# A woven scan and feed-forward stage: weights in eight spaced pieces, two GELUs and a spare square root, other banks and block order

## The reference

```
def step(S, inp):                       # 64 chunks of 16 tokens, per head, D = 16
    kh = k @ S;  target = v - k
    kh_hat = (kh - mean(kh)) * rsqrt(var(kh) + EPS)
    g = w * kh_hat + b - target;  gw = g * w
    v_new = (gw - mean(gw) - kh_hat * mean(gw * kh_hat)) * rstd
    A = tril(q @ k.T) * eta
    qh = q @ S - A @ v_new
    o = q + layernorm(qh, w, b)
    S = S - (k * eta).T @ v_new
x = x + rmsnorm(o * sigmoid(gate)) * norm_w @ Wo
x = x + (gelu(x @ Wg.T) * (x @ Wu.T)) @ Wd.T     # MLP_DIM 2048, x of 2048 tokens
```

## Time and profile before

| | us |
|---|---|
| median of 3 runs (lowest, highest) | 3264.78 (3262.69, 3271.79) |
| profiled execution, its own time | 3264.96 |
| its span, first to last instruction | 3262.9 |

### The profile page before, as it was taken

One profiled execution on the slowest core, in us unless ns is written; L12 is line 12 of the kernel. 1 busy time (PEld: TensorE's weight loads), 2 busy tenths in 40 slices (PEclk: granted clock), 3 DMA queues, 4 the chain that ended last, 5 costly groups with the idle time before them and its releaser, 6 DMA issues. The chain is left out here.

```text
span 3262.9 us, 69524 instructions
## 1 busy us (share of the span) xinstructions
PE 2505.6 (77%) x25665; PEld 1674.5 (51%) x25752; DVE 2174.5 (67%) x4949; ACT 1820.7 (56%) x3501; POOL 851.8 (26%) x870
## 2 busy tenths in 40 slices
PE   7788869878888787676776777699987035888889
PEld 3333327533333663344443444478865034777789
DVE  7488886758785766898998999743335335555552
ACT  3398864324445432898998999632223002666664
POOL 2233333200000412454554555200002101222223
PEclk9899989869999888899999999899988555888889
DMA  3533311253231224222201220030000794112210
GB/s 124 124 65 64 64 66 50 91 90 53 42 37 15 96 93 110 32 27 28 27 11 19 27 27 1 9 152 1 1 14 11 157 193 53 25 26 31 38 27 11
DMA packets 300472, 173.95 MB, mean 53 GB/s; under 512 B 206961, under 2 KB 265345, under 8 KB 297857
## 3 DMA queue, kind: packets, MB, share of 16 engines
q1 hardware_dynamic: 290560, 156.69, 24.2%
q10 hardware_dynamic: 9600, 13.13, 1.3%
HBM read 113.84 MB, written 51.51 MB: 51 GB/s over the span
## 5 line engine op out<-in xcount | busy, mean ns | idle before, releaser
L1279 ACT ACTIVATE ad_e<-ps,ad_nm 128x1024 f32<-128x1024 f32 (+7 forms) x512 | 384.2, 758 | 92.6 <-DVE ad_nm L1340 90.5
L1340 DVE TENSOR_REDUCE ad_nm<-ps 128x1 f32<-128x1024 f32 (+7 forms) x512 | 369.2, 749 | 49.6 <-PE ps L1210 49.0
L1313 POOL TENSOR_TENSOR ad_e<-ad_e,ad_c 128x128 f32<-128x128 f32 (+7 forms) x256 | 293.3, 1146 | 15.1 <-DVE ad_rz L1353 8.7
L1208 PE MATMUL ps<-ad_k_st,ad_q_st 96*128 96x512 bf16 (+3 forms) x768 | 211.8, 336 | 91.9 <-ACT ad_e L1279 49.5
L615 ACT ACTIVATE ab_e<-ps 128x512 f32<-128x512 f32 (+3 forms) x384 | 167.6, 490 | 204.7 <-PE ps L532 158.8
L1364 DVE CUSTOM_DVE_ANT_0 ad_t<-ad_e,ad_rz 128x128 f32<-128x128 f32 (+7 forms) x256 | 224.0, 875 | 3.7 <-ACT ad_pr L1287 2.5
L365 PE MATMUL ps<-warm,ident_b 128*128 128x512 bf16 x425 | 137.4, 389 | 114.5 <-ACT ad_prT L1264 112.1
L1306 POOL TENSOR_TENSOR ad_e<-ad_e,later_k 128x128 f32<-128x128 f32 x256 | 118.7, 464 | 374.5 <-ACT ad_e L1279 374.5
L1898 POOL TENSOR_TENSOR st_it_low<-st_it,st_it_high 128x256 fp32r<-128x256 f32 x128 | 95.3, 745 | 416.0 <-ACT st_it_high L2069 371.1
L1287 ACT ACTIVATE ad_pr<-ad_t,ad_low 128x128 f32<-128x128 f32 (+7 forms) x256 | 200.7, 784 | 0.0
L1223 PE MATMUL ps<-ident,ad_pr 128*128 128x128 f32 x1152 | 174.0, 279 | 24.5 <-ACT ad_pr L1287 24.5
(11 more groups left out here) (387 smaller groups left out, 7097.7 us busy)
## 6 DMA issues: line engine op xcount, KB each, us to landing
aa_q_st<-scr_a SPq DMA_DIRECT2D x48, 256.0 KB, 6.2
split<-f_split SPq DMA_DIRECT2D x16, 768.0 KB, 3.9
ad_q_st<-scr_d SPq DMA_DIRECT2D x48, 256.0 KB, 9.7
g_w<-split SPq DMA_DIRECT2D x8, 1536.0 KB, 18.5
st_w<-split ACTq DMA_DIRECT2D x8, 1536.0 KB, 21.7
scr_a<-pa_parts SPq DMA_DIRECT2D x24, 384.0 KB, 2.5
scr_d<-pd_parts SPq DMA_DIRECT2D x20, 384.0 KB, 2.5
aa_k_st<-scr_a SPq DMA_DIRECT2D x48, 128.0 KB, 6.5
```

The source lines that it names most:

```text
L1208: last = pe.matmul(m.ps[:, bank, 0:n], q_st[:, b, 2 * h + s, t * P:(t + 1) * P], k_st[:, b, s, cc * QB:cc * QB + n], start=True, stop=True)
L1279: act.activation(e[:, u % EB, s, 0:L], src, ACT.Exp, bias=nm[:, u % EB, s:s + 1], accum_out=z[:, u % EB, s:s + 1]).then_inc(exped[s], 1)
L1313: pool.tensor_tensor(e[:, k, 1, 0:L], e[:, k, 1, 0:L], c[:, k:k + 1].to_broadcast([P, L]), ALU.mult).then_inc(mixed, 1)
L1340: dve.tensor_reduce(nm[:, u % EB, s:s + 1], src, AX.X, ALU.max, negate=True).then_inc(maxed[s], 1)
```

## The change

`DENSE` goes from 21 to 19 and block work moves to lags 5 to 12. The weights are issued one piece every second step, from step 3 on. Both GELUs of a step follow each other, behind the scan's square root; a spare square root of a constant (`keep_table`) follows them. The roots of the block work stand next to a square root. On the PE the order is gate, gate, up, down, up, and `project_down(1)` comes ahead of the scan's key product; banks and their waits follow that order. On DVE `finish` comes first in its step, and the odd multiply moves from ahead of `gradient` to just ahead of `advance`. `statistics` is cut out of `add_rows` and comes late in the step. `wo` and `norm_w` are loaded behind the first scan inputs, with their own semaphore.

```diff
-    DENSE = 21
+    DENSE = 19
...
+    kept_root = ph.sb("kept_root", [P, 1])
...
-    bank_of = lambda product: 3 + product % 3
+    bank_of = lambda r, part: 3 + (4 * (r // 2) + 2 * part + r % 2) % 3
...
-    sp.dma_start(wo[:], a["wo_t"].rearrange("(k p) n -> p k n", p=P)).then_inc(w_loaded, 16)
-    sp.dma_start(g_row[:], a["norm_w"].rearrange("(k x) -> k x", k=2).partition_broadcast(P)).then_inc(w_loaded, 16)
+    sp.dma_start(wo[:], a["wo_t"].rearrange("(k p) n -> p k n", p=P)).then_inc(wo_loaded, 16)
+    sp.dma_start(g_row[:], a["norm_w"].rearrange("(k x) -> k x", k=2).partition_broadcast(P)).then_inc(wo_loaded, 16)
...
-    pool.wait_ge(w_loaded, 48)
+    pool.wait_ge(wo_loaded, 32)
...
-    in_turns(pool, [(DENSE + 1, remainder(1)), (14 - 7, at_block_end(gain_and_base)), (15 - 7, at_block_end(weigh)),
-                    (DENSE, remainder(0))], NCH)
+    in_turns(pool, [(6, at_block_end(gain_and_base)), (6, at_block_end(weigh)),
+                    (DENSE, remainder(0)), (DENSE, remainder(1))], NCH)
...
-        if part == 0:
-            reach(pe, gated, r - 1)
+        if (part, r % 2) == (0, 0):
+            reach(pe, gelued, r)
+        elif (part, r % 2) == (0, 1):
+            reach(pe, gated, r - 2)
+        elif (part, r % 2) == (1, 0):
+            reach(pe, gated, r)
-            out = m.ps[:, bank_of(2 * r + part), 0:TB]
+            out = m.ps[:, bank_of(r, part), 0:TB]
...
-    def gate_even(n):
-        hidden(2 * n, 0, gate)
-    def up_even(n):
-        hidden(2 * n, 1, up)
-    def both_odd(n):
-        hidden(2 * n + 1, 0, gate)
-        hidden(2 * n + 1, 1, up)
+    def first_product(odd):
+        return lambda n: hidden(2 * n + odd, 0, gate)
+    def second_product(odd):
+        return lambda n: hidden(2 * n + odd, 1, up)
...
+        if j == 0:
+            pe.wait_ge(wo_loaded, 32)
...
-    pe.wait_ge(w_loaded, 48)
-    in_turns(pe, [(2, update), (2, within_chunk), (DENSE, gate_even), (1, state_keys), (1, state_queries), (0, early),
-                  (17 - 7, at_block_end(project_out)),
-                  (DENSE, up_even), (DENSE + 2, project_down(1)), (DENSE, both_odd), (DENSE + 1, project_down(0)),
-                  (16 - 7, at_block_end(turn_rows)), (19 - 7, at_block_end(turn_normed))], NCH)
+    in_turns(pe, [(2, update), (2, within_chunk), (DENSE + 2, project_down(1)),
+                  (1, state_keys), (1, state_queries), (0, early),
+                  (8, at_block_end(turn_rows)), (9, at_block_end(project_out)),
+                  (DENSE, first_product(0)), (DENSE, first_product(1)), (DENSE, second_product(0)),
+                  (DENSE + 1, project_down(0)), (DENSE, second_product(1)),
+                  (11, at_block_end(turn_normed))], NCH)
...
-            act.activation(ge[:, r % 2, :], m.ps[:, bank_of(2 * r), 0:TB], ACT.Gelu_apprx_tanh).then_inc(gelued, 1)
+            act.activation(ge[:, r % 2, :], m.ps[:, bank_of(r, 0), 0:TB], ACT.Gelu_apprx_tanh).then_inc(gelued, 1)
...
+    def load_weights(n):
+        if n % 2 == 0 and n // 2 < MLP // C:
+            act.dma_start(w[:, n // 2].bitcast(F32), a["split"][n // 2]).then_inc(w_in[n // 2], 16)
+    def keep_table(n):
+        reach(act, table_kept, n)
+        act.activation(kept_root[:], eps[:, 0:1], ACT.Sqrt).then_inc(table_kept, 1)
-    for c in range(MLP // C):
-        act.dma_start(w[:, c].bitcast(F32), a["split"][c]).then_inc(w_in[c], 16)
-    in_turns(act, [(2, copy), (13 - 7, at_block_end(square_rows)), (15 - 7, at_block_end(square_again)),
-                   (20 - 7, at_block_end(keep_high_x)),
-                   (DENSE, gelu(0)), (1, square), (1, square_root), (DENSE + 1, keep_high(1)), (DENSE, gelu(1)),
-                   (DENSE, keep_high(0)),
-                   (13 - 7, at_block_end(root_rows)), (15 - 7, at_block_end(root_again)), (16 - 7, at_block_end(copy_rows)),
-                   (18 - 7, at_block_end(root_x)), (19 - 7, at_block_end(scale_second))], NCH)
+    in_turns(act, [(2, copy), (5, at_block_end(square_rows)),
+                   (1, square), (1, square_root), (7, at_block_end(root_again)), (11, at_block_end(scale_second)),
+                   (DENSE, gelu(0)), (DENSE, gelu(1)), (DENSE, keep_table),
+                   (5, at_block_end(root_rows)), (10, at_block_end(root_x)), (6, at_block_end(square_again)),
+                   (DENSE, keep_high(0)), (DENSE, keep_high(1)),
+                   (8, at_block_end(copy_rows)), (11, at_block_end(keep_high_x)),
+                   (3, load_weights)], NCH)
...
-    dve.wait_ge(w_loaded, 48)
+    dve.wait_ge(w_loaded, 16)
...
-            dve.tensor_tensor(it[:, r % 2, :], ge[:, r % 2, :], m.ps[:, bank_of(2 * r + 1), 0:TB],
+            dve.tensor_tensor(it[:, r % 2, :], ge[:, r % 2, :], m.ps[:, bank_of(r, 1), 0:TB],
...
+    def statistics(j):
...
-    in_turns(dve, [(13 - 7, at_block_end(sum_rows)), (14 - 7, at_block_end(normalise_rows)), (15 - 7, at_block_end(sum_again)),
-                   (16 - 7, at_block_end(size_rows)), (18 - 7, at_block_end(add_rows)), (19 - 7, at_block_end(scale_first)),
-                   (20 - 7, at_block_end(keep_low_x)),
-                   (1, receive), (1, variance), (DENSE + 1, multiply(1)), (1, gradient), (0, mask),
-                   (DENSE + 2, at_block_end(finish)), (DENSE, multiply(0)), (1, advance)], NCH)
+    in_turns(dve, [(DENSE + 2, at_block_end(finish)), (6, at_block_end(normalise_rows)), (7, at_block_end(sum_again)),
+                   (8, at_block_end(size_rows)), (10, at_block_end(add_rows)), (11, at_block_end(scale_first)),
+                   (12, at_block_end(keep_low_x)),
+                   (1, receive), (1, variance), (1, gradient), (DENSE, multiply(0)), (0, mask),
+                   (5, at_block_end(sum_rows)), (10, at_block_end(statistics)),
+                   (DENSE, multiply(1)), (1, advance)], NCH)
```

More of the change, by code:

```diff
@@ L1778, in scan_and_ffn @@
     it_low = ph.sb("it_low", [P, 4, TB], F32R)
-    made, cleared, w_loaded = ph.sem("made"), ph.sem("cleared"), ph.sem("w_loaded")
+    made, cleared, w_loaded, wo_loaded = ph.sem("made"), ph.sem("cleared"), ph.sem("w_loaded"), ph.sem("wo_loaded")
     rows_in = [ph.sem(f"rows_in{k}") for k in range(len(EDGES) - 1)]
@@ L1795, in scan_and_ffn @@
                                                         ph.sem("n_scaled_a"), ph.sem("n_turned"))
-    x_high_in, x_low_in = ph.sem("x_high_in"), ph.sem("x_low_in")
+    x_high_in, x_low_in, table_kept = ph.sem("x_high_in"), ph.sem("x_low_in"), ph.sem("table_kept")
     gate, up, gelued, gated = ph.sem("gate"), ph.sem("up"), ph.sem("gelued"), ph.sem("gated")
```

## The result

The changed kernel takes 3188.88 us (median of 4 runs, 3187.07 to 3195.24) against 3268.28 of the kernel before (4 runs); the ratio is 0.9761, 95% interval 0.9737 to 0.9785: 79 us faster. Forecast were 3160 us and a range of 3120 to 3212. The execution profiled took 3195.24 us, its span is 3193.2.

The account below looks back on a forecast made before the run. Losses were put less in the plain step than in block work and the clock, with the PE as the bound afterwards. Middle part -82, tail -6.5 and weights -18 sum to -106.5 from 3264.96: 3160 us, 8 in 10 within 3120 to 3212.

Parts of the forecast that it names:

- (b): Woven steps: the chain bounds and the plain step stays 6.95 us; 3190 us, chance 0.20 together with (e).
- (e): Only block work (finish and roots) gains, plain step and early part stay; 3192 us, chance 0.20 together with (b).
- Plain step: Woven step without block work: falls from 6.95 to 6.3 us, the PE becoming the bound.
- Woven part: The 46 steps from 18th to 64th state advance: 337 against 419.4 us, -82; 58.6 us a block including clock.
- 0.7 for small waits: Term in the woven part's block sum of 56.6 us: 0.7 us a block for small waits.
- Weights: First part of the stage: spaced weight pieces and earlier rows give -18 us, bounds -31 and 0.
- I keep 10 of the 13 us: First part: 10 us of loss for weights remains with spaced pieces, since the traffic is the same.
- 2 relay: First part: 2 us of loss left for the relay, the 14.81 us step shrinking to 5 to 7.
- Tail: Dense work after the scan: -8.6 for two fewer steps, +4 as ACT bounds, -2 for block roots; -6.5 us.
- (a): Woven steps: the clock stays low for half of them, 67 us instead of 11.5; 3215 us, chance 0.16.
- (c): First part: ACT is held by its own weight issues, 120 us; 3280 us, chance 0.05 together with (d).
- (d): Woven part and tail: ACT drains at each table switch, 122 us more; 3282 us, chance 0.05 together with (c).

Follow-up runs that it names:

- small gain ops: Changed kernel with POOL's multiply by gain and addition of base cut to 4 of 128 columns, a cost probe only: 3176.26 us, ratio 0.9727.
- six profiles with the same woven part: Profiles of the changed kernel, its repeat, and its edits of weights, rows and tail, woven part unedited: woven 347.5 to 352.4 us.

## Why the prediction was right, and where it was off

The mechanism of the woven part was right. The total, 29 us off, is less good than the wide range makes it look: the parts measured +1.7, -67.8 and -5.8 add up to -72, against -106.5. It landed beside the numbers of rivals (b) and (e), 3190 and 3192 us, of which neither happened; that is chance.

- *Plain step, right.* 6.3 us with the PE as the bound; the root's wait (0.36 left) and the remainder's overlap gone, the multiply and the advance hidden as argued. The advance keeps 0.22 us beside a remainder, the lower of the two bounds.
- *Woven part, -82 forecast, -67.8 measured.* The mechanism held (block roots without loads, 29.5 us alone on the kernel before; no wait for `finish`). A block took 61.1 us on the mean instead of 58.6, which is the 14 us. Two terms were mis-sized. One is the clock: "I take two such steps in three blocks: 2 us a block" allowed 11.5 us. The PE was busy 327.1 us; a block at full clock keeps it busy 53.35 us (steps 33 to 40, with step 53's 6.09 in place of step 37), which is 306.8 in all, so the low clock took an estimated 20 us. The other is the "0.7 for small waits": the PE's idle time was 24.5 us where the sum had 3.2 a block, 18.4 in all, and 15.6 of it were waits for the PE's own instructions, which the sum names only for the start of the stage. The gap after POOL's ops, called 1.5 us, was 1.6 to 1.8 and right; that it costs the clock of the next step was not in the sum, and small gain ops show that it does.
- *Weights, -18 forecast, about +2 measured.* This is the step that failed: "I keep 10 of the 13 us" and "2 relay". The PE's waits for instructions rose from 31.2 to 39.6 us in the first part, and spacing the weights is what made them longer (33.3 without it). The step that waits for the relayed rows was to shrink to 5 to 7 us and grew to 18.15. I had put the `rows` issues some 30 us earlier without asking what the weights between them do to their length, which went from 33 to 47 us; so the relay began only 10 us earlier, while ACT, with block work one step earlier in its program, came to wait for it 10 us earlier too. That this move costs time in the first part is read from the traces; no run has it alone. Spacing alone gave 5.3 us, and the rest of the change took 7.0. The issue of 15.48 us in the earlier trace rows was also not the only one held: the next took 14.20 us.
- *Tail, -6.5 forecast, -5.8 measured*, by two errors of opposite sign, so its nearness is luck: ACT does not bound it (spare root 0.20 us, not 0.30; GELUs 0.66, not 0.76), and the PE idles 10.2 us where it idled 5.9, most of it in the block work of the last blocks.
- *DENSE.* I booked two tail steps at 4.28 us as gain. With DENSE back at 21 the tail takes 5.5 us again and the woven part loses 12 to 16, an unknown part of it by a luckier clock; in this order the shorter lag showed no gain.
- *Rivals.* (a) came part of the way: the mean clock of the woven part is 0.92, so 16% of it is at the low level. (b) is out: the plain step takes 6.30 us and the chain doesn't bound it. (c) is out at 0.34 us a piece. (d) is out: the two GELUs start 1.29 us after their load. (e) is out, since the plain step gained; but block work was indeed a large part, 29.5 us for its roots alone.

How the 67.8 us split among the parts is only partly shown. On the kernel before, block roots give 29.5; in the changed one, the spare root gives 12 to 16. For the rest, some 25 us, there are only the traces: the waits for `finish` (21.5 us in the earlier trace rows) and the remainder's overlap are gone. The orders of the PE and DVE lists, the places of POOL's ops and the lags of the block work were not tried one by one.

## What to carry to other kernels

Place an engine's rare operations where its function table is already loaded; here it was worth more (29.5 us, on the kernel before) than a spare load in each step (12 to 16, in the changed kernel). When work is moved ahead in an in-order queue, count what now stands ahead of the critical operation: `project_down(1)` beside the gate product made the plain step 7.67 us, and without it there the step is 6.30, though that kernel differs in more than this. Spread long operations that contend with the critical chain over steps with slack, and look at the length of other queues' issues before calling a transfer's new place free.

## What was not expected of the hardware

- 24 issues of `rows` (68 or 102 KB each) held SP's queue for 33 to 35 us, and for 47 us with weight pieces of 1.5 MB issued between them.
- A gap of 1.5 to 1.8 us in an otherwise full PE stretch at the end of a step was followed by a low clock in 29 of 30 blocks over six profiles with the same woven part; a step then takes 8.9 instead of 6.1 us. Gaps of 1.06 to 1.43 us in the middle of a step were followed by it too.
- In the woven part, with a DMA share of 0.23, 15.6 us of the PE's idle time have no releaser in the profile (read here as waits for its own instructions), more than all waits for other engines.
- ACT's spare square root of one column takes 0.20 us, against 0.30 for the scan's with scale and bias, and two GELUs in a row take 0.66 us, not 0.76.
